# Attention's sums via DRAM, divided feature-major per eight heads

## What is computed

```
x = x + 0.5 * ffn(layernorm(x))        # softmax over tokens, top 2 of 8 experts, three layers
x = x + attention(layernorm(x))        # causal, 16 heads of 16
x = x + 0.5 * ffn(layernorm(x))
attention: q, k, v = x @ w_qkv.T;  probs = softmax(mask(q @ k.T / 4));  (probs @ v) @ w_out.T
```

## Time and profile before

| | us |
|---|---|
| median of 3 runs | 2114.99 |
| lowest and highest run | 2114.93, 2117.0 |
| the profiled execution | 2126.23 |
| its span | 2124.5 |
| mean granted clock | 0.975 |

### The profile page before, as it was taken

One profiled execution on the slowest core, in us unless ns is written; L12 is line 12 of the kernel. 1 busy time (PEld: TensorE's weight loads), 2 busy tenths in 40 slices (PEclk: granted clock), 3 DMA queues, 4 the chain that ended last, 5 costly groups with the idle time before them and its releaser, 6 DMA issues.

```text
span 2124.5 us, 99858 instructions
## 1 busy us (share of the span) xinstructions
PE 2047.7 (96%) x43659; PEld 1584.0 (75%) x43659; DVE 1817.7 (86%) x4023; ACT 1598.6 (75%) x3311; POOL 414.5 (20%) x1118
## 2 busy tenths in 40 slices
PE   5899989999999999999999999999999999879998
PEld 3788866377877777777787777777778776658885
DVE  6666666899999999999999999999999994676665
ACT  5344446599999999999999999999999998334442
POOL 1333213411121111121111111111111111023330
PEclk8899989999999999999999999999999999979998
DMA  8211103300010000100001001000010002231112
GB/s 273 74 47 50 42 16 125 134 30 25 13 34 14 25 30 8 34 20 18 31 7 33 22 16 34 9 29 27 11 34 16 22 4 69 54 118 47 45 49 88
DMA packets 70394, 94.36 MB, mean 44 GB/s; under 512 B 16640, under 2 KB 59396, under 8 KB 69956
## 3 DMA queue, kind: packets, MB, share of 16 engines
q1 hardware_dynamic: 62796, 68.75, 10.1%
q0 software_dynamic: 6816, 19.20, 3.4%
q10 hardware_dynamic: 344, 0.01, 0.0%
HBM read 62.24 MB, written 25.43 MB: 41 GB/s over the span
## 4 chain that ended last, share of the span: by engine, by line
PE 88%; DVE 6%; issue 2%; ACT 1%; POOL 1%; DMA 1%; SPq 1%; another core or an unknown queue 0%; DVEq 0%; ACTq 0%; POOLq 0%
PE bank L1264 39%; PE bank L1257 22%; PE bank L1139 17%; PE bank L1346 3%; PE bank L1150 1%; PE bank L1375 1%; DVE stats L1405 1%; PE bank L1307 1%; PE bank L1157 1%; DVE rows L1427 1%; DVE x_res L1725 1%; SPq L698 0%; POOL work L591 0%; DVE work L1594 0%; PE bank L1217 0%
## 5 line engine op out<-in xcount | busy, mean ns | idle before, releaser
L966 ACT ACTIVATE feat<-bank 128x512 f32<-128x512 f32 (+3 forms) x2304 | 1263.2, 565 | 113.8 <-PE bank L1264 13.3
L1264 PE MATMUL bank<-work 96*32 96x512 bf16 (+2 forms) x15872 | 1206.4, 370 | 5.0 <-DVE work L1772 3.8
L1772 DVE TENSOR_REDUCE work<-bank 128x1 f32<-128x512 f32 (+1 forms) x1920 | 1178.9, 659 | 26.4 <-PE bank L1264 23.4
L1257 PE MATMUL bank<-feat,phase 128*17 128x128 f32 (+3 forms) x18432 | 879.2, 263 | 0.3 <-ACT feat L972 0.3
L1257 PEld LDWEIGHTS bank<-feat,phase 128*17 128x17 f32 x18432 | 588.4, 98 | 270.7 <-ACT feat L972 13.7
L1264 PEld LDWEIGHTS bank<-work 96*32 96x32 bf16 (+1 forms) x15872 | 472.6, 96 | 57.1 <-DVE work L1772 24.6
L1139 PE MATMUL bank<-work 128*128 128x256 f32 (+1 forms) x1872 | 398.4, 363 | 0.6 <-issue 0.2
L1139 PEld LDWEIGHTS bank<-work 128*128 128x128 f32 x1872 | 325.1, 192 | 37.1 <-issue 1.0
L625 POOL TENSOR_SCALAR_AFFINE_SELECT feat<-feat 128x128 f32<-128x128 f32 x512 | 145.1, 292 | 456.0 <-ACT feat L966 439.1
L1656 DVE COPY work<-phase 128x514 f32 x234 | 101.5, 436 | 124.1 <-ACT work L880 99.5
L578 POOL DMA_INDIRECT work<-token_table,row_no x142 | 138.1, 973 | 299.0 <-PE bank L1150 142.6
(11 more groups left out here) (201 smaller groups left out, 1371.9 us busy)
## 6 DMA issues: line engine op xcount, KB each, us to landing
phase<-in_w SPq DMA_DIRECT2D x12, 1024.0 KB, 12.0
work<-qk_parts SPq DMA_DIRECT2D x60, 192.0 KB
token_table<-rows SPq DMA_DIRECT2D x8, 1056.0 KB, 8.7
work<-work SPq DMA_DIRECT2D x512, 0.5 KB
qk_parts<-phase SPq DMA_DIRECT2D x20, 384.0 KB, 2.8
work<-qk_parts SPq DMA_DIRECT2D x60, 128.0 KB
qk_parts<-work SPq DMA_DIRECT2D x12, 384.0 KB, 2.8
x_res<-in_x SPq DMA_DIRECT2D x8, 512.0 KB
```

The lines of the kernel that those rows point to most:

```text
L966: eng.activation(p_ring[:, n % P_RING, lo:QB], s_bank("probs", n)[:, lo:QB], ACT.Exp, scale=HD ** -0.5).then_inc(sig.s_done, 1)
L1257: mm = eng.matmul(bank[ACC_BANK][GRID * g:GRID * g + VW, GRID * i0:P], v_aug[:, t, h, :], weights[:, i0:TPJ, g, :], start=(t == 0), stop=( ...
L1264: mm = eng.matmul(out[GRID * g:GRID * (g + 1), width], left[:, GRID * g:GRID * (g + 1)], right, start=start, stop=stop)
L1772: eng.tensor_reduce(maxima[:, h % 2, j, PLACE[i], at:at + 1], scores[:, 0:hi - lo], AX_X, ALU.max).then_inc(sig.a_done, 1)
```

## The change

ACT's copy of a unit's sums is now stored to DRAM as it is (`sums_dram`, head by 32 rows by token; 16 rows are features, the 17th the totals). Only when the eighth head of a half (h = 7 or 15) finishes a block j, five steps follow, each set so many items after its `acc` (`DIVIDE_STEPS`): SP loads the totals of eight heads as 128 x 32, DVE inverts them, SP stores the reciprocals, SP loads the sums of eight heads feature-major (128 features by 512 tokens) and the reciprocals, repeated for 16 features, in the same form, and DVE multiplies the two. `heads` then has features on partitions, as the product with w_out wants them; head transposes and their copies are gone. The last unit's reciprocal and product stand in DVE's `attended`, after the 4th and the 8th pair.

The groups g of 32 queries leave attention in their own order, so x is regrouped on the host by 32 tokens within 512, and the second norm's copy into `feat` (n = 1) puts the tokens back. The third norm's rows lie in `work`, the second routing's one-hot tables in `rows`. The loads of the second ffn's weights wait for the last division, since reciprocals lie in `phase`.

```diff
@@ -82,7 +84,9 @@
...
-PV_LAG, PV_PAUSE, TURN_LAG, DIVIDE_LAG = 5, 1, 2, 2
+PV_LAG, PV_PAUSE, STORE_LAG = 5, 1, 2
+LAST_RECIPROCALS, LAST_DIVIDE = 8, 16
+DIVIDE_STEPS = (("load_totals", 7), ("reciprocals", 14), ("store_reciprocals", 16), ("load_parts", 21), ("divide", 30))
@@ -216,9 +220,6 @@
...
-        while unturned and unturned[0][0] <= n:
-            yield "turn", unturned[0][1]
-            undivided.append((n + DIVIDE_LAG, unturned.pop(0)[1]))
@@ -227,22 +228,23 @@
...
+                later.append((n + STORE_LAG, "store_sums", h * NJ + j))
+                if h % HEADS_PER_PART == HEADS_PER_PART - 1:
+                    later += [(n + lag, what, h * NJ + j) for what, lag in DIVIDE_STEPS]
+                later.sort()
                 pause = PV_PAUSE + 1
                 break
...
-        while undivided and undivided[0][0] <= n:
-            yield "divide", undivided.pop(0)[1]
+        while later and later[0][0] <= n:
+            yield later.pop(0)[1:]
     while summed < ITEMS:
         yield "pv", summed
         summed += 1
     yield "acc", len(UNITS) - 1
-    for _, u in unturned + [(ITEMS, len(UNITS) - 1)]:
-        yield "turn", u
-        undivided.append((ITEMS, u))
-    for _, u in undivided:
-        yield "divide", u
+    later += [(ITEMS, "store_sums", len(UNITS) - 1)] + [(ITEMS + lag, what, len(UNITS) - 1) for what, lag in DIVIDE_STEPS]
+    for _, what, u in sorted(later):
+        yield what, u
...
@@ -444,13 +454,13 @@
...
-        recip = carve(2 * TPJ).rearrange("p (b i) -> p b i", b=2)
-        sums = carve(2 * TPJ * GRID).rearrange("p (b i w) -> p b i w", b=2, i=TPJ)
+        totals = carve(2 * TOTALS).rearrange("p (b c) -> p b c", b=2)
...
+        recips = [phase[:, at_v + j * QB:at_v + (j + 1) * QB] for j in range(NJ - 1)] + [spare[:, QB:2 * QB]]
...
@@ -458,7 +468,31 @@
...
-        heads = rows[:, :, 0:D]
+        heads = rows[:, :, :].rearrange("p i r -> p (i r)")[:, 0:KD * S].rearrange("p (k s) -> p k s", k=KD)
+        late_rows = work[:, 0:NT * ROW].rearrange("p (i r) -> p i r", i=NT)
+
+        def rows_of(f):
+            return late_rows if f else rows
...
+        def summed_of(h, j):
+            return heads[:, h // HEADS_PER_PART, j * QB:(j + 1) * QB]
+
+        def recips_of(h, j):
+            return recips[j] if h // HEADS_PER_PART else heads[:, 1, j * QB:(j + 1) * QB]
+
+        def units_of(h, j):
+            return slice(h - HEADS_PER_PART + 1, h + 1), slice(j * QB, (j + 1) * QB)
+
+        def divisions(h, j):
+            return h // HEADS_PER_PART * NJ + j + 1
@@ -624,11 +658,6 @@
...
-                    elif what == "divide":
-                        h, j = UNITS[n]
-                        need.wait_ge(sig.recip, n + 1)
-                        eng.tensor_tensor(heads[:, TPJ * j:TPJ * (j + 1), h * HD:(h + 1) * HD], sums[:, n % 2, :, 0:HD],
-                                          bc(recip[:, n % 2, :], 2, [P, TPJ, HD]), ALU.mult).then_inc(sig.divided, 1)
@@ -646,6 +675,7 @@
             def load_experts(f):
                 if f == 1:
                     need.wait_ge(sig.pv, PV_ALL)
+                    need.wait_ge(sig.divided, KD * NJ)
 ...
@@ -717,6 +747,30 @@
...
+                elif what == "store_sums":
+                    h, j = UNITS[n]
+                    need.wait_ge(sig.acc, n + 1)
+                    eng.dma_start(sums_dram[h, :, j * QB:(j + 1) * QB].rearrange("w (g c) -> g w c", g=TPJ),
+                                  acc_out[:, n % 2, :]).then_inc(sig.sums_stored[n % 2], 16)
+                elif what == "load_totals":
+                    h, j = UNITS[n]
+                    heads_of, tokens = units_of(h, j)
+                    need.wait_ge(sig.sums_stored[n % 2], 16 * (n // 2 + 1))
+                    eng.dma_start(totals[:, j % 2, :], sums_dram[heads_of, HD, tokens]).then_inc(sig.totals_loaded[j % 2], 16)
+                elif what == "store_reciprocals":
+                    h, j = UNITS[n]
+                    heads_of, tokens = units_of(h, j)
+                    need.wait_ge(sig.recip, divisions(h, j))
+                    eng.dma_start(recips_dram[heads_of, tokens], totals[:, j % 2, :]).then_inc(sig.recips_stored[j % 2], 16)
+                elif what == "load_parts":
+                    h, j = UNITS[n]
+                    heads_of, tokens = units_of(h, j)
+                    need.wait_ge(sig.recips_stored[j % 2], 16 * of_parity(h, j))
+                    if h >= HEADS_PER_PART:
+                        need.wait_ge(sig.divided, divisions(h - HEADS_PER_PART, j))
+                    eng.dma_start(summed_of(h, j), sums_dram[heads_of, 0:HD, tokens]).then_inc(sig.parts_loaded[j % 2], 16)
+                    eng.dma_start(recips_of(h, j), recips_dram[heads_of, tokens].unsqueeze(1).to_broadcast(
+                        [HEADS_PER_PART, HD, QB])).then_inc(sig.parts_loaded[j % 2], 16)
@@ -771,8 +825,11 @@
...
-                        eng.activation(feat[:, k, i0 * P:(i0 + 4) * P], bank[k][:, :],
-                                       ACT.Copy).then_inc(sig.feat[n], 1)
+                        to, of = feat[:, k, i0 * P:(i0 + 4) * P], bank[k][:, :]
+                        if n == 1:
+                            to = to.rearrange("p (i g b) -> p g i b", i=TPJ, g=TPJ)
+                            of = of.rearrange("p (g i b) -> p g i b", i=TPJ, g=TPJ)
+                        eng.activation(to, of, ACT.Copy).then_inc(sig.feat[n], 1)
...
@@ -968,24 +1022,8 @@
...
-                        need.wait_ge(sig.turned, n - 1)
+                        need.wait_ge(sig.sums_stored[n % 2], 16 * (n // 2))
                         eng.activation(acc_out[:, n % 2, :], bank[ACC_BANK][:, 0:P], ACT.Copy).then_inc(sig.acc, 1)
@@ -1349,32 +1386,18 @@
...
-            def transpose_heads(n):
-                need.wait_ge(sig.a_done, len(A_ITEMS))
-                need.wait_ge(sig.divided, len(UNITS))
-                for k in range(KD):
-                    m = n * KD + k
-                    need.wait_ge(sig.heads_copy, m - len(H_BANKS) + 1)
-                    for i in range(4 * n, 4 * n + 4):
-                        eng.transpose(bank[H_BANKS[m % len(H_BANKS)]][:, (i - 4 * n) * P:(i - 4 * n + 1) * P],
-                                      rows[:, i, k * P:(k + 1) * P], ident[:, :]).then_inc(sig.heads_tr, 1)
-
             def attended(g):
-                for n in range(2 * g, 2 * g + 2):
-                    if n == 0:
-                        transpose_heads(0)
-                    if n + 1 < NT // 4:
-                        transpose_heads(n + 1)
-                    for i2 in range(4 * n, 4 * n + 4, 2):
-                        need.wait_ge(sig.heads_copy, KD * (n + 1))
...
+                for i2 in range(g * LN_GRP[2], (g + 1) * LN_GRP[2], 2):
+                    need.wait_ge(sig.divided, divisions(H - 1, i2 // TPJ))
+                    need.wait_ge(sig.a_done, len(A_ITEMS))
+                    need.wait_ge(sig.acc, len(UNITS))
+                    need.wait_ge(sig.attended, i2 // 2 - 1)
...
+                            eng.matmul(bank[bk][:, (i - i2) * D:(i - i2 + 1) * D], heads[:, k, i * P:(i + 1) * P],
@@ -1422,9 +1445,9 @@
                 if n == 1:
                     need.wait_ge(sig.table[0], 16 * GROUPS)
                 if n == 2:
-                    need.wait_ge(sig.heads_tr, 4 * KD * 2 * (g + 1))
+                    need.wait_ge(sig.s_full, S_ALL)
...
@@ -1645,6 +1668,8 @@
...
+                if f == 1:
+                    need.wait_ge(sig.table[f], 16 * GROUPS)
...
@@ -1731,9 +1756,21 @@
...
-                for i2 in range(g * GRP, (g + 1) * GRP, 2):
+                for i2 in range(g * LN_GRP[2], (g + 1) * LN_GRP[2], 2):
                     need.wait_ge(sig.out_mm, KD * (i2 + 2))
                     add_pair(i2, 4 + i2 // 2 % 2, sig.attended)
+                    if i2 + 2 == LAST_RECIPROCALS:
+                        reciprocals(*UNITS[-1])
+                    if i2 + 2 == LAST_DIVIDE:
+                        divide(*UNITS[-1])
+
+            def reciprocals(h, j):
+                need.wait_ge(sig.totals_loaded[j % 2], 16 * of_parity(h, j))
+                eng.reciprocal(totals[:, j % 2, :], totals[:, j % 2, :]).then_inc(sig.recip, 1)
+
+            def divide(h, j):
+                need.wait_ge(sig.parts_loaded[j % 2], 32 * of_parity(h, j))
+                eng.tensor_tensor(summed_of(h, j), summed_of(h, j), recips_of(h, j), ALU.mult).then_inc(sig.divided, 1)
@@ -1782,15 +1819,10 @@
...
-                    elif what == "turn":
-                        need.wait_ge(sig.acc, n + 1)
-                        need.wait_ge(sig.divided, n - 1)
-                        eng.transpose(sums[:, n % 2].rearrange("p i w -> p (i w)"),
-                                      acc_out[:, n % 2, :]).then_inc(sig.turned, 1)
-                    elif what == "divide":
-                        need.wait_ge(sig.turned, n + 1)
-                        need.wait_ge(sig.divided, n - 1)
```

(17 more changed lines are left out.)

80 lines of the change are left out of this document (35 added, 45 removed).

## The result

The changed kernel takes 2155.8 us (median of 4 runs, 2153.3 to 2158.0), the kernel before on the same chip 2115.9 (2114.9 to 2117.0). The ratio is 1.0189, with a 95% interval of 1.0174 to 1.0204: 39.9 us slower. The forecast was 2113.7 us, and its range ended at 2120.5.

What follows compares the result with a forecast made beforehand. PE was taken to bound attention, with DVE close behind, and a chain to bound the seam. Attention +2.5 us and seam -3.8 us gave -1.3 us, off the median 2114.99: 2113.7 us, range 2109.0 to 2120.5.

Steps and rivals of the forecast that it cites:

- PE is the bound in an ordinary head: Attention: PE runs at 97% of its own rate, DVE close behind; less DVE work per unit gains only 0.3 us.
- DVE's added work: Heads 7 and 15: added reciprocals and products exceed DVE's free time, costing 1.7 us and 1.1 us.
- Queues cost 0: ACT, SP and POOL queues and the second norm's regrouped copies: added stores, loads and waits have slack, cost 0.
- Rival D: All heads: the store's wait in SP's order delays max rows, PE idles 0.5 us each, 2121.7 us; chance 0.04.
- The chain of a division: Sums and totals through DRAM: store and load of totals fit in 8.5 us, parts' load takes 4.4, 0.6 to spare.
- rival C: Head 7: division loads land late behind stack loads, DVE and PE wait; 2120.3 us, at worst +26 (2139); chance 0.17.
- Head 15: Last head of attention: only five units' added DVE work counts, costing 1.1 us.
- The seam: Between attention and third norm: head transposes vanish, but pauses and clock falls take some back; net -3.8 us.
- -5.0 to the first statistics: Start of the seam: output products start right after the acc copy, so the third norm's statistics come 5.0 us sooner.
- Last division and second pause: Seam, second group: last division adds 0.6, later transposes give 0.6; PE's pause grows to 4.6 us, costing 1.7 as before.
- Third pause: Seam, before the tenth pair: a new PE pause of 2.8 us costs 1.7 with a clock fall, 0 without; taken 1.2.

Runs made afterwards that it cites:

- all_later: The changed kernel with all division steps of head 7 set more items after the acc copy and a totals buffer per unit; 2122.8 us.
- pool_divides: all_later with head 7's eight 128x512 products on POOL instead of DVE; 2123.4 us.
- before_again: The kernel before the change, unedited, profiled a second time; 2117.5 us.
- both_later: all_later with later division steps for units 0 to 4 of head 15 too; 2119.5 us.
- no_stack_8: The changed kernel without the load of head 8's q and k during head 7 (head 8 works with those of head 6); 2140.0 us.
- split_stacks: The changed kernel with each stack load issued as one transfer per part of 16 rows, 24 instead of 12 a head; 2143.9 us.
- four_banks: both_later with the third norm's output products going through four PSUM banks instead of two; 2108.2 us, ratio to the kernel before 0.9955.

## Why the prediction was wrong, point by point

*PE is the bound in an ordinary head*: right, 86.7 us with one turn and one reciprocal less per unit. A gain of 0.3 us in all cannot be seen. (The sum of DVE's needs comes to 1111 us, not 1112, which changes nothing.)

*DVE's added work*: right in kind. The 128x32 reciprocal takes 346 ns, the forecast had 466 (and the lower bound 187), the product 687 as taken from the earlier trace rows. The effect, forecast at 1.7 us in head 7, is 1.1 (all_later; 1.0 of it the products, by pool_divides), and in head 15 0.7 with later steps (1.1 forecast).

*Queues cost 0*: ordinary heads lose nothing to 128 stores, and the second norm's regrouped copies nothing visible (the first acc copy ends 125.1 us after the second norm's first statistics begin, before_again has 124.8). Rival D did not occur.

***The chain of a division*: this step failed.** It said: "Store and load of totals, 2 x 2.8 us, fit in 8.5" and "4.4 us, 0.6 to spare". Two errors stand in it. First, the size: the loads of parts take 5.3 to 5.8 us alone, not 4.4, and rival C's own condition was over 5. With 5 us given, each is late before anything else is in the queue; head 15 shows that price, 2.5 us more than the 0.7 of both_later, and no_stack_8 shows it in head 7. By rows the error was at the rate taken from one window and a start of 1.5 us; the stores and loads of this chain show that even 16 to 64 KB take 1.9 to 2.4. Secondly, and larger, the chain was summed as if its queue were empty. SP's queue has a stack load every 6 items in head 7 as in every head but the last. The 2.8 us were read as the time that one holds its engines, but they are the width of the window chosen in the earlier trace rows; in that same trace the load lands 5.0 us after its issue, and 8.0 behind two part loads in the changed kernel. I put this into rival C as a lateness at "three such units" and 6.6 us; the trace has DVE standing 8 times, 28.3 us in all. Nor was it asked what comes behind a late step: the next unit's store goes out behind the same queue (5.64 us behind a stack load, then 7.81 behind two part loads and a stack load), so lateness is passed on. C's far price of 26 us was the nearer one. How the lateness divides between the queue on the engines and SP's waiting in order stays open.

*The clock in attention* was no term anywhere. Pauses of 2.4 to 4.3 us in PE were followed by half-clock stretches, 37.5 us in all between 1037.9 and 1164.2 us, and two thirds again was added to PE's idle time. My own reading of the seam had this mechanism; it belonged into rival C too.

*Head 15* was forecast at +1.1 and cost 3.2, by the same failed step.

*The seam*: forecast -3.8 us, measured -2.4 (50.2 to 47.8). Step by step: -5.0 to the first statistics, measured -4.95. Last division and second pause, +0.6 - 0.6: measured +0.88 (groups 14.35 us apart, 13.47 before), with a longer pause (4.91 us, forecast 4.6) and a longer half-clock stretch, 1843.44 to 1850.27, where before it was 3.4 us. Third pause, +1.2: measured +1.65, a full fall. The order of events was right, the falls were undercounted by 1.3. The size is in part luck: in the seven other kernels of the table whose seam is that of the change, acc end to fourth statistics takes 47.4 to 49.0 us, so the gain is between 1.2 and 2.8. PE's second and third pause are 4.9 and 3.0 us in them too, but behind the same 4.9 us the clock stays at half for 6.8 us in the change and both_later and for 3.4 in all_later and pool_divides. The length of the pause alone does not set the price. None of them reaches 3.8.

The Trainium skill ("DMA: Bandwidth & Descriptors", why a DMA increments its semaphore by 16) was cited for the engines that a transfer gets by its slowest dimensions. split_stacks agrees in direction: with a leading 16 instead of 3 the same bytes land in 3.3 instead of 5.3 us. The engines seem rightly counted: in the trace the semaphore of a part load gets 9 updates, that of a stack load with leading 3 gets 4 and with leading 16 gets 16, which fits 8, 3 and 16 engines and, where they are fewer than 16, one update at the start. The time was wrong, since it was scaled from a window of another transfer. From the Trainium skill ("VectorE: DVE Perf Modes", the fixed hardware budget: reciprocal repeats its divide step 8 times) the forecast had worked out an estimate of 8.3 ns a column; from 202 ns for 8 columns to 346 for 32 the trace has 6.0.

## What to carry to other kernels

A value that goes out to DRAM and comes back in several hops must be planned by measured issue-to-landing times, each hop with everything else that its queue carries at that time in front of it; where lateness can be bought off, put the consumer late (here the product 76 items instead of 30 behind its sums, and the steps between them later too, saved 36 of 38 us). An in-order engine that is nearly as full as the bound is the worst place to wait, and its lost time counts more than once, since the clock of TensorE fell behind the pauses (here 22.5 us of idle PE became 38 us). When a change frees a resource, here two PSUM banks, look what waits for that resource elsewhere: here four banks were worth 11 us, more than the change itself.

## What the runs showed of the hardware

A wait of the feeding engine cost more than its length: 22.5 us of idle PE came with 15.5 us of slower matmuls, at half clock in stretches of 3.4 to 17 us. The same pause of 4.9 us at the seam was followed by 3.4 us at half clock in two kernels and by 6.8 in others.

A transfer's time depends on what was issued before it on the same queue, even where the mean DMA share is only 0.18 (head 7) of the engines: the 64 KB store took 2.4 us alone, 5.6 behind a 192 KB load of leading dimension 3, 4.5 behind two loads of 256 KB (no_stack_8) and 7.8 behind all three.

POOL multiplies 128x512 in 1.28 us, DVE in 0.69; run in POOL's gaps it did not lengthen DVE's reductions (682 ns in pool_divides, 680 in all_later).

One stall has no releaser: in pool_divides PE stood 0.93 us in unit 3 of head 8 (below, its weight loads), at the same unit in which all_later and both_later lose 0.6 to 1.0. In the trace's packets the instruction load of 16 KB before it comes 7.1 us after the last one, where they are otherwise 3.4 to 5.6 apart between 1091 and 1150 us, and the parts and stack loads are in the queues between. The other kernels fit: at this place both_later has 6.3 us between instruction loads and a stall of 0.51, all_later 7.0 and 0.96, four_banks 7.1 and 1.05, before_again at most 5.0 and no stall. That instruction loads stand behind data is what this suggests; it was not tried.

```profile
1126.79 0.09 PEld L1298 LDWEIGHTS bank<-feat,phase 128*17 128x17 f32 x1 [0.93 <-issue]
```
